# Another order of VectorE's and GpSimd's work in a software-pipelined gated delta rule

## What is computed

```python
q, k, v = x @ Wq.T, x @ Wk.T, x @ Wv.T
q, k, v = (_causal_dwconv(t, w, b) for ...)      # depthwise, 4 taps
g    = jax.nn.log_sigmoid(x @ Wg.T)
beta = jax.nn.sigmoid(x @ Wb.T)
k = k / jnp.clip(jnp.linalg.norm(k, axis=-1, keepdims=True), 1e-12, None)
def step(S, inp):                                # over the 2048 tokens
    q_t, k_t, v_t, g_t, b_t = inp
    Sk = jnp.einsum('bhkv,bhk->bhv', S, k_t)
    delta = jnp.einsum('bhv,bhk->bhkv', v_t, k_t) - jnp.einsum('bhv,bhk->bhkv', Sk, k_t)
    S = jnp.exp(g_t)[..., None, None] * S + b_t[..., None, None] * delta
    o_t = jnp.einsum('bhkv,bhk->bhv', S, q_t)
```

## Time and profile before

| | |
|---|---|
| median of 3 runs | 1883.41 us (1879.09 to 1884.63) |
| the profiled execution | 1890.86 us, its span 1888.9 us |
| TensorE (PE) busy | 1621.4 us, 86% of the span |
| VectorE (DVE) busy | 1302.2 us, 69% |
| GpSimd (POOL) busy | 1068.5 us, 57% |
| ScalarE (ACT) busy | 669.4 us, 35% |
| mean granted TensorE clock | 0.956 of full speed |

### The profile page before, as it was taken

One profiled execution on the slowest core, in us unless ns is written; L12 is line 12 of the kernel. 1 busy time (PEld: TensorE's weight loads), 2 busy tenths in 40 slices (PEclk: granted clock), 3 DMA queues, 4 the chain that ended last, 5 costly groups with the idle time before them and its releaser, 6 DMA issues. The chain is left out here.

```text
span 1888.9 us, 72945 instructions
## 1 busy us (share of the span) xinstructions
PE 1621.4 (86%) x31244; PEld 1239.6 (66%) x31244; DVE 1302.2 (69%) x3029; ACT 669.4 (35%) x1290; POOL 1068.5 (57%) x1261
## 2 busy tenths in 40 slices
PE   7479999999999999999999999776999995798950
PEld 6236666666666666666666666665888885787840
DVE  1388999999999999999899999623555553222214
ACT  1244444444444444444444444211111211233313
POOL 0155565565565565655556556412777776577853
PEclk9799999999999999999999999988999998899985
DMA  6245555555555546555545545425554551699557
GB/s 264 84 83 108 109 110 119 120 111 117 123 107 122 121 102 122 113 109 115 122 109 110 118 111 106 89 53 178 165 172 148 173 149 52 186 252 224 95 93 234
DMA packets 530210, 245.39 MB, mean 130 GB/s; under 512 B 423504, under 2 KB 497872, under 8 KB 528992
## 3 DMA queue, kind: packets, MB, share of 16 engines
q1 hardware_dynamic: 443872, 204.95, 43.5%
q0 software_dynamic: 18432, 18.99, 5.8%
q10 hardware_dynamic: 67584, 16.79, 4.0%
HBM read 169.29 MB, written 71.37 MB: 127 GB/s over the span
## 5 line engine op out<-in xcount | busy, mean ns | idle before, releaser
L373 PE MATMUL delta_p_j<-delta_xt,delta_w 128*128 128x512 f32 x768 | 389.2, 630 | 30.0 <-DMA delta_xt<-in_xt 17.4
L572 DVE SCALAR_TENSOR_TENSOR delta_kq<-delta_hist,cw,delta_kq 128x512 f32<-128x512 f32 x384 | 367.6, 957 | 32.6 <-ACT delta_kq L718 23.6
L711 ACT ACTIVATE delta_hist<-delta_p_j 128x512 f32<-128x512 f32 x192 | 114.9, 599 | 473.2 <-PE delta_p_j L373 464.9
L373 PEld LDWEIGHTS delta_p_j<-delta_xt,delta_w 128*128 128x128 f32 x768 | 132.5, 192 | 145.8 <-issue 112.3
L1220 POOL DMA_INDIRECT slot_tokens<-mix_tokens,mix_slot x192 | 189.9, 989 | 62.4 <-issue 61.8
L860 POOL TENSOR_TENSOR delta_sd<-state,eg_end 128x256 f32<-128x256 f32 x128 | 104.9, 820 | 203.1 <-DVE state L652 203.1
L586 DVE SCALAR_TENSOR_TENSOR delta_yv<-delta_hist,cw,delta_yv 128x512 f32<-128x512 f32 x128 | 166.3, 1299 | 7.5 <-ACT delta_yv L718 5.3
L434 PEld LDWEIGHTS delta_p_i<-delta_kkq,rt 64*64 64x64 f32 x4096 | 130.5, 135 | 59.1 <-issue 44.0
L492 PEld LDWEIGHTS delta_p_c<-delta_r,delta_kkq 64*64 64x64 f32 x2048 | 70.9, 136 | 125.1 <-DVE delta_r L644 71.3
L1343 DVE SCALAR_TENSOR_TENSOR expert_gate<-expert_gate,expert_p_h 88x256 f32<-88x256 f32 x64 | 26.7, 417 | 176.9 <-ACT expert_gate L1363 176.9
L434 PE MATMUL delta_p_i<-delta_kkq,rt 64*64 64x32 f32 (+1 forms) x4096 | 141.6, 213 | 4.5 <-DVE delta_kkq L636 3.8
(11 more groups left out here) (145 smaller groups left out, 3699.5 us busy)
## 6 DMA issues: line engine op xcount, KB each, us to landing
delta_xd<-x_scratch SPq DMA_DIRECT2D x256, 128.0 KB, 4.4
delta_w<-in_wqkv SPq DMA_DIRECT2D x64, 416.0 KB
w<-in_w SPq DMA_DIRECT2D x64, 352.0 KB
delta_eg<-eg_rows SPq DMA_DIRECT2D x128, 130.0 KB
n_scratch<-delta_kkq ACTq DMA_DIRECT2D x128, 128.0 KB
mix_ot<-ot SPq DMA_DIRECT2D x16, 1024.0 KB, 5.7
w<-in_w SPq DMA_DIRECT2D x64, 176.0 KB
ot<-delta_o SPq DMA_DIRECT2D x32, 256.0 KB
```

The costliest lines, as they stand in the source:

```text
L373: mm = pe.matmul(p_j[:, :], w[e][:, (ch * 3 + n) * 128:(ch * 3 + n) * 128 + 128], xt[m // 8 % 2][:, ch * 512:ch * 512 + 512], start=ch == ...
L572: ve.scalar_tensor_tensor(out, view(hist[e], i * 2 * 518 + tap, (259, 2), (1, 256)), cw[:, column:column + 1], out, ALU.mult, ALU.add).the ...
L711: ac.activation(view(hist[e], n * 518 + 3, (259, 2), (1, 256)), p_j[:, :], ACT.Copy)
```

## The change

On VectorE, `conv` gets an argument with the taps to take, and the list of a slot is written in another order. In both kinds of slot, `residual(two_)` moves up to stand behind the first of the three passes of k's convolution. In an odd slot the rows 0 to 5 of the substitution, which stood partly ahead of and partly behind `residual(two_)`, become rows 0 to 8: three behind `lengths`, and six behind `update(two_)`, with the second Horner step of the slot behind them and `conv_values` last. In an even slot the rows 6 to 10 become rows 9 and 10, ahead of `update(one)`; rows 11 to 14 stay.

On GpSimd, `scale_values` is split: the power (now `roots`) stays as the last instruction of a slot, and the scaling of the values comes in the next slot, behind `decay_state(one)` and `off_diagonal`; `carry_in` comes behind it.

```diff
-            def conv(m, i, tapped, done):
+            def conv(m, i, tapped, done, taps=(2, 1, 0)):
...
-                for tap in (2, 1, 0):
+                for tap in taps:
...
                 if even:
-                    substitute(subst_group, range(6, 9))
+                    substitute(subst_group, range(9, 11))
                 if one:
                     update(*one)
                 if is_macro(m):
-                    conv(m, 0, tap_k, conv_k)
-                if even:
-                    substitute(subst_group, range(9, 11))
-                if odd:
-                    substitute(subst_group, range(0, 2))
+                    conv(m, 0, tap_k, conv_k, (2,))
                 if two_:
                     residual(*two_)
+                if is_macro(m):
+                    conv(m, 0, tap_k, conv_k, (1, 0))
                 if is_macro(before):
                     lengths(before)
                 if even:
                     substitute(subst_group, range(11, SUB - 1))
                 if odd:
-                    substitute(subst_group, range(2, 6))
+                    substitute(subst_group, range(0, 3))
                 if is_macro(before):
                     inverse_lengths(before)
                 if is_macro(mi):
                     horner(mi, rx_done, 16, y1_out)
                 if two_:
                     update(*two_)
-                if is_macro(m):
-                    conv_values(m)
-                if is_macro(mi):
-                    horner(mi, ry1_done, 32, y2_out)
+                if odd:
+                    substitute(subst_group, range(3, 9))
+                    if is_macro(mi):
+                        horner(mi, ry1_done, 32, y2_out)
+                    if is_macro(m):
+                        conv_values(m)
+                else:
+                    if is_macro(m):
+                        conv_values(m)
+                    if is_macro(mi):
+                        horner(mi, ry1_done, 32, y2_out)
                 if is_macro(before):
                     mask(before)
...
+            def roots(m):
+                if m >= 1:
+                    po.wait_ge(vp_out, m)
+                po.tensor_tensor(root[:, :], n2[:, :], view(s.half_power, 0, (0, 8)), ALU.pow).then_inc(small, 1)
+
             def scale_values(m):
-                po.tensor_tensor(root[:, :], n2[:, :], view(s.half_power, 0, (0, 8)), ALU.pow).then_inc(small, 1)
                 po.wait_ge(small, m + 1)
...
-                if is_macro(m):
-                    carry_in(m)
                 if one:
                     decay_state(*one)
                 if is_macro(mi):
                     off_diagonal(mi)
+                if is_macro(t - 2):
+                    scale_values(t - 2)
+                if is_macro(m):
+                    carry_in(m)
...
-                    scale_values(before)
+                    roots(before)
```

## The result

The changed kernel takes 2012.38 us (median of 4 runs, 2004.52 to 2016.59) where the kernel before takes 1884.02: the ratio is 1.0656, 95% interval 1.0615 to 1.0697. The forecast was 1937 us with a range to 1966: the direction was right, and the rise of 128 us is more than twice the 54 that were forecast.

A forecast was written before the change was run, and what follows sets the result against it. VectorE, with almost no idle time, was taken to set the pace. Odd slots +2.95 and even -0.95 gave +2.0 us a pair, 1.9 was taken, and 28.5 pairs gave +54 us: 1937 us, range 1892 to 1966.

The forecast's parts named there:

- VectorE's order is the pace: Slots 7 to 62: VectorE has almost no idle time and TensorE waits for it about once a pair.
- Six rows behind the update, +3.4 us: Odd slot: short row instructions behind update(two) each wait out a large GpSimd instruction, +3.4 us, the largest term.
- Values, k and q freed, -1.25, -0.25 and -1.1: Passes free of GpSimd: values in odd slots -1.25 us, k in both slots -0.25, q in even slots -1.1.
- The stall at the residual in odd slots, +1.25: Odd slot: VectorE's early residual waits for TensorE's products from `chain_state(two)`, +1.25 us.
- The idle 3 us of TensorE: Odd slot: TensorE idles 3 us before the third inverse product, waiting for the late Horner step; costs VectorE nothing.
- the stall of "about 0.2": Even slot: VectorE waits about 0.2 us for the products the early residual needs, +0.2.
- the places laid end to end: New slot lengths, odd 21.75 and even 15.93 us, 37.7 a pair, 1.7 over the mean pair of 36.04.
- Slots before 7 and after 64, 0: Slots outside the stretch have idle time on VectorE, so the change costs 0 there.
- The bounds: Limits for what no row shows: a pair changes by between -0.3 and +3.4 us.
- the short instructions that slip through: Rival: row instructions pass between GpSimd's without losing a turn, pair -0.3 us, 1875 us; chance 0.12.
- the power that blocks as well: Rival: rows also wait beside GpSimd's power, about 1.1 us more a pair, 1968 us; chance 0.05.
- TensorE's pace: Rival: TensorE sets the pace, its 1.33 us of even-slot waits go, pair 34.7 us, 1846 us; chance 0.06.

The follow-up runs named there:

- Taking TensorE's waits for the residual away: Kernel before, with the residual of the second chain step behind k's first pass in even slots only: 1894.37 us, ratio 1.0008.
- giving VectorE's passes their free time: Kernel before, with GpSimd's power moved from behind the keys to right behind the clipping: 1864.79 us, ratio 0.9856.
- the filler of wide products: Changed kernel plus 11 unused products (128x128 by 128 columns) on TensorE before the last inverse product of odd slots with a chain: 1955.71 us, ratio 1.0316.
- the kernel with two of them out: Changed kernel with the second Horner step behind three rows, not six, and the early residual in even slots only: 1935.13 us, ratio 1.0224.

## Why the prediction was half right

Taken in the order of its steps.

*VectorE's order is the pace.* Right. Taking TensorE's waits for the residual away gave 1.0008, and giving VectorE's passes their free time gave 0.9856. One reading was too narrow: the 5.1 us of the earlier trace rows are the mask's wait alone, and VectorE's waits for TensorE's products between 500 and 1000 us are 11.8 in all.

*Six rows behind the update, +3.4 us.* Right in mechanism and size. The five long row instructions cost 0.87 + 0.97 + 0.67 + 0.92 + 0.97 less five times 0.22, which is 3.3. In the trace 145 row instructions are over 0.3 us, as against 2 before, and 133 of them lie in the 28 odd slots, four or five in each. Over the 28 pairs the row instructions take 259.8 us after 172.3, which is 3.1 a pair.

*Values, k and q freed, -1.25, -0.25 and -1.1.* Right: 1.53, 2.27 (0.74 and 1.53) and 2.32.

*The stall at the residual in odd slots, +1.25.* Right in kind, too small on the mean. In the odd slot shown it is 0.80, since TensorE took 5.1 us from `chain_solve(one)` to the products and not the 5.66 of the row with a DMA gap. But the same place is also where a late DMA of the inverse now lands: in odd slots with such a gap the residual waits up to 4.4 us, and the odd slots of 24 us come of it. So the residual waits 1.76 us on the mean of the 28 odd slots, and the mean odd slot is 22.04 where a quiet one is 21.1. On the kernel before, the early residual in both kinds of slot costs 1.1 an odd slot.

*The idle 3 us of TensorE, "this costs VectorE nothing".* This is the step that failed. The idle time itself was forecast well (3 us, measured 2.97 in the slot shown), and then priced by VectorE's need for the last inverse product alone, at the duration that TensorE's work had in rows taken at full clock. The runs showed that the clock is at 0.50 when TensorE resumes, and that the chain of the even slot, with the stall of "about 0.2", waits for it: 1.7 to 2.2 us at the residual and up to 1.0 at the update. With the clock kept up by a filler the even slot is 16.01 (15.93 forecast), its residual waits 0.25 on the mean, and a pair is 37.92, against the 37.7 of the places laid end to end and the 37.9 of the forecast with 1.9 added. So the term that was put at nothing is 2.17 us a pair, and the rest of the sum holds. That it holds to 0.02 us is luck in part: the 0.2 from 37.7 to 37.9 was a choice, and a stall that was too small stands against rows that were a little too dear.

*Slots before 7 and after 64, 0.* Wrong for the last ones. Slots 63 to 69 took 11.3 us more, of which the forecast counted about 1 with its half pair. Slot 63 took 5.5 of it, slot 65, where only two row instructions are long, 4.7, and slot 66 2.0. The clock falls in these slots in the kernel before, in the changed one and in the one with the filler of wide products, and in the last they took 11.4 us more all the same; what makes them longer is open.

54 forecast and 61 for the clock make 115, the last slots 10, and all else took 3.6 less: 121, the growth of the span. The medians differ by 128.

*The bounds.* They do not follow from their own terms. Three of the five waits at 1.49 in place of 0.95 add 1.6 to the 3.4, which is 5.0 and not 4.5, and a pair of +3.4 comes to 1980 us, above the 1966 at which the range was closed. Neither reaches 2012, for the clock was in no bound.

Of the rivals, the short instructions that slip through did not appear, and the power that blocks as well did not either: the rows beside it take 0.22. TensorE's pace is answered above.

What stays open: the even slots are of two kinds, 13 of 17.2 to 17.3 us and 15 of 18.2 to 18.8, and the second kind stands each time behind the longer stretch of half clock; what makes that stretch long or short I did not look into. The overlap of the costs in the kernel with two of them out is told by its waits but not tested.

## What to carry to other kernels

Price the idle time that a new order gives to TensorE, even where nobody waits for it: here what followed 1.7 to 3.0 us of it ran at half clock in every odd slot, and as a chain went through it, the price was that of the chain. Do not put a train of short dependent VectorE instructions with two SBUF inputs beside a train of large GpSimd instructions, for here each paid what was left of a whole one of the other (0.67 to 0.97 us for 0.22); a long one pays the same once for more work. Put GpSimd's long instructions on small tiles, such as the power here, where VectorE's short ones run, and its large ones beside VectorE's reads of PSUM (the update of the state takes 0.41 us beside `ex` and 0.41 alone).

## What the runs showed of the hardware

The clock fell to the 1.2 GHz level behind 4.79 us of back-to-back products of 16 columns that left no gap in the record, as it did behind 3.0 us of idle time, and stayed at 2.4 GHz behind 2.72 us of products of 128x128 by 128 columns in the same place. The Trainium skill (TensorE: Matmul & The Clock Gate, the part on the clock gate) says that how busy the array has been sets which of the two levels it gets. The trace agrees on the idle time and on the wide products; the narrow ones show that an engine that is busy by the record can lose its clock all the same.

A power of 128x8 takes 2.11 us when a convolution pass is under way at its start, as in 58 of the 64 of the kernel before (2.11 at 576.50), and 1.67 in the other six and where a row is under way (1.67 at 582.67 after). The passes and rows inside it run free. It looks as if the power waits once at its start and keeps nothing from VectorE after that; no run tests this by itself.
